# Graph attention by row chains over 128 runs of consecutive edges instead of one-hot matmuls over items

## What is computed

```python
h = x @ W                                    # per node, 256 wide
e = leaky_relu(al_s[src] + al_d[dst], 0.2)   # a score per edge and head
m = segment_max(e, dst)
ex = exp(e - m[dst])
denom = segment_sum(ex, dst)
out = segment_sum(h[src] * ex / denom[dst], dst) + b
```

## Time and profile before

| | us |
|---|---|
| median of 3 runs | 7049.85 |
| lowest and highest run | 7016.26 and 7051.68 |
| span of the profiled execution | 7015.4 |
| attention, layer 1 (1659 to 4269) | 2610 |
| close_first | 148 |
| attention, layer 2 (4417 to 6911) | 2494 |
| close_last | 105 |

### The profile page before, as it was taken

One profiled execution on the slowest core, in us unless ns is written; L12 is line 12 of the kernel. 1 busy time (PEld: TensorE's weight loads), 2 busy tenths in 40 slices (PEclk: granted clock), 3 DMA queues, 4 the chain that ended last, 5 costly groups with the idle time before them and its releaser, 6 DMA issues. The chain is left out here.

```text
span 7015.4 us, 84308 instructions
## 1 busy us (share of the span) xinstructions
PE 4539.2 (65%) x21954; PEld 3343.3 (48%) x21954; DVE 4230.7 (60%) x11585; ACT 2593.8 (37%) x7475; POOL 3741.4 (53%) x3828
## 2 busy tenths in 40 slices
PE   6776999995555555555555558466666666666662
PEld 4554777774444444444444445344444444444441
DVE  8997876665555555555555558555555555555557
ACT  7983222221444444444444446222222222222221
POOL 1334432233666666666666660566666666666661
PEclk9998999997777777777777779677777777777776
DMA  9997343333434434444444444444434344333446
GB/s 338 373 376 286 115 155 114 110 113 95 115 113 120 116 114 117 117 118 116 113 119 116 114 118 131 120 116 115 118 112 117 113 118 118 113 115 112 118 116 237
DMA packets 391446, 997.85 MB, mean 142 GB/s; under 512 B 106626, under 2 KB 199094, under 8 KB 378502
## 3 DMA queue, kind: packets, MB, share of 16 engines
q0 software_dynamic: 175200, 469.15, 24.7%
q1 hardware_dynamic: 205798, 471.33, 19.5%
q10 hardware_dynamic: 10048, 52.70, 1.9%
HBM read 804.88 MB, written 187.99 MB: 142 GB/s over the span
## 5 line engine op out<-in xcount | busy, mean ns | idle before, releaser
L247 POOL DMA_INDIRECT rows<-table_d,idx x3328 | 3217.8, 967 | 2077.7 <-issue 884.9
L489 DVE TENSOR_TENSOR acc<-acc,pG 128x264 f32 (+1 forms) x3328 | 1414.1, 425 | 1928.5 <-DMA rows_d<-begin_e 890.8
L290 PE MATMUL pG<-rows,onehot 128*128 128x264 f32 (+1 forms) x6656 | 2357.3, 502 | 308.7 <-issue 226.6
L290 PEld LDWEIGHTS pG<-rows,onehot 128*128 128x128 f32 x6656 | 1543.7, 248 | 922.4 <-issue 568.4
L350 ACT ACTIVATE onehot<-pQ 128x1024 f32<-128x1024 f32 (+1 forms) x512 | 442.4, 864 | 2223.5 <-DMA g2b<-in_g_b 1562.6
L357 ACT ACTIVATE rows<-rows 128x64 f32<-128x64 f32 (+1 forms) x4480 | 1251.4, 367 | 4.2
L264 PE MATMUL pQ<-k_nrow,drow 128*128 128x128 bf16 x3328 | 326.5, 248 | 638.9 <-ACT onehot L350 636.9
L271 PE MATMUL pS<-adt,onehotT 128*128 x3328 | 294.7, 171 | 544.7 <-issue 533.7
L264 PEld LDWEIGHTS pQ<-k_nrow,drow 128*128 128x128 bf16 x3328 | 250.0, 111 | 658.4 <-ACT onehot L350 647.5
L945 PE MATMUL pH<-hT_pre,w1h 128*128 128x256 f32 x1568 | 412.5, 419 | 137.9 <-ACT hT_pre L805 111.9
L271 PEld LDWEIGHTS pS<-adt,onehotT 128*128 128x128 bf16 x3328 | 219.1, 97 | 573.7 <-issue 535.0
(11 more groups left out here) (323 smaller groups left out, 5131.2 us busy)
## 6 DMA issues: line engine op xcount, KB each, us to landing
onehotT<-drow_d SPq DMA_DIRECT2D x128, 832.0 KB
ea<-in_ea SPq DMA_DIRECT2D x98, 768.0 KB
rows_d<-run SPq DMA_DIRECT2D x97, 768.0 KB
rows<-table_d,idx POOLq DMA_INDIRECT x3328
pre_d<-pre ACTq DMA_DIRECT2D x49, 1024.0 KB
pre_in<-pre_d SPq DMA_DIRECT2D x49, 1024.0 KB
hrow_c<-table_d SPq DMA_DIRECT2D x98, 256.0 KB
tab<-tab_d SPq DMA_DIRECT2D x64, 260.0 KB
```

Of the source, the lines that this page charges most:

```text
L247: g.indirect_dma_start(out=rows[:, at.par, k, 0:XF + H], out_offset=None, in_=table, in_offset=bass.IndirectOffsetOnAxis(ap=idx[:, at.par, ...
L290: mm = pe.matmul(pG[(k + 2 * at.par) % 4][:, 0:W], onehot[:, k, :], rows[:, at.par, k, :], start=True, stop=True)
L489: v.tensor_tensor(to, to, pG[(k + 2 * at.par) % 4][:, 0:W], ALU.add).then_inc(added, 1)
```

## The change

Both attention layers are computed in another way, and what only the old way needed goes.

**The layout.** Partition p gets the edges p*1563 to p*1563 + 1562, so step k of a "row chain" handles one edge in each of the 128 runs. The 1563 steps are cut into 58 groups: 23, then 54 of 28, then 14, 7 and 7. `rows` is a ring of four slots of one group each.

**The steps of a group.** POOL gathers one column of 128 rows per step (1563 gathers per layer, the index column in SBUF for good) and waits once per group, for the slot. DVE `maxima` computes the scores, a forward and a backward scan per head for the maximum, and the exponent. ACT takes the exponential. The rows are weighed: in layer 1, 20 of 28 by DVE in fours, both inputs in SBUF, and 8 by ACT; in layer 2 all by ACT. Then DVE `chain_rows`: one scalar_tensor_tensor per step, running row = running row before * same + row, read from one PSUM bank and written to the next, in a ring of six banks, each behind the one before. ACT copies two banks at a time back over the rows in SBUF, and SP stores the group to HBM (`sums1`, `sums2`). The last edge of a node then holds its sum.

**Ends of runs.** A node that spans a border of two runs is fixed at the end of the layer: the last rows of all runs go through small matmuls, and one indirect gather and one scatter mend the first node of each run.

**Around it.** `acc` in SBUF is gone: `close_first` and `close_last` fetch the sums from HBM with 98 gathers each (`Shares`), in chunks of 14 tiles with two buffers, and the softmax division moves into the chunks. The destination scores are scattered to the first edge of each node (98 small scatters in `node_mlp` for layer 1, 98 in `close_first` for layer 2, after the arrays are zeroed) and spread along the run by a scan. Item lists, tables and their stores are gone from `edge_chains` and `node_mlp`; PE has nearly no work in `attention`. The table rows carry 2H scores.

The core of the diff:

```diff
+GROUP = 28
+TAPER = (14, 7, 7)
+SLOTS = 4
...
+        body = self.EA - sum(TAPER)
+        sizes = [body % GROUP] * (body % GROUP > 0) + [GROUP] * (body // GROUP) + list(TAPER)
+        self.groups = []
+        for n, size in enumerate(sizes):
+            self.groups.append(Group(n, sum(sizes[:n]), size, sizes))
...
+    by_vector = [0 if H == 1 else min(g.size // 4 * 4, 4 * max(1, round(0.72 * g.size / 4))) for g in groups]
+    duos = [-(-g.size // 2) for g in groups]
+    first_duo = [sum(duos[:g.n]) for g in groups]
+    by_scalar = [g.size - n for g, n in zip(groups, by_vector)]
...
+            for g in groups:
+                sp.wait_ge(copied, first_duo[g.n] + duos[g.n])
+                sp.dma_start(outv[:, g.first * W:g.end * W],
+                             rows[:, g.slot, 0:g.size, :].rearrange("p k w -> p (k w)")).then_inc(stored[g.slot], 16)
...
+                if g.use:
+                    p.wait_ge(stored[g.slot], 16 * g.use)
+                    p.wait_ge(zm_ready, g.n - SLOTS + 2)
+                    p.wait_ge(fa_ready, g.n - SLOTS + 1)
+                for k in range(g.size):
+                    e = g.first + k
+                    p.indirect_dma_start(
+                        out=rows[:, g.slot, k, :], out_offset=None, in_=table,
+                        in_offset=bass.IndirectOffsetOnAxis(ap=keep["src"][:, e:e + 1], axis=0),
...
+                left = list(range(by_vector[g.n], g.size))
+                ahead = 4 if H == 1 else 0
+                for k in left[:ahead]:
+                    weigh(k)
+                left = left[ahead:]
+                for d in range(duos[g.n]):
+                    n = min(2, g.size - 2 * d)
+                    a.wait_ge(chained, min(g.first + 2 * d + 3, g.end))
+                    bank = (first_duo[g.n] + d) % 3 * 2
+                    a.activation(here[:, 2 * d:2 * d + n, 0:V], pC[:, bank:bank + n, 0:V], ACT.Copy).then_inc(copied, 1)
+                    for k in left[:2]:
+                        weigh(k)
+                    left = left[2:]
+            a.wait_ge(exponents, 2)
+            a.activation(flows[:, :, :], flows[:, :, :], ACT.Exp).then_inc(flows_ready, 1)
+            a.activation(old[:, :], old[:, :], ACT.Exp).then_inc(flows_ready, 1)
...
+            def destination_scores():
+                v.wait_ge(first_in, 16)
+                v.wait_ge(own_in, 16)
+                link(v.tensor_copy(ad[:, 0, :], own[:, V:W]))
+                for h in range(H):
+                    link(v.tensor_tensor_scan(ad[:, :, h], keep["same"][:, :], ad[:, :, h], 0.0, ALU.mult, ALU.add))
...
+            def maxima(g):
+                here, n = rows[:, g.slot, 0:g.size, :], g.size
+                prev = rows[:, groups[g.n - 1].slot, groups[g.n - 1].size - 1, :]
+                v.wait_ge(gath_in[g.slot], g.landed)
+                link(v.tensor_tensor(z[:, 0:n, :], here[:, :, XF:V], ad[:, g.first:g.end, :], ALU.add))
+                link(v.scalar_tensor_tensor(out=z[:, 0:n, :], in0=z[:, 0:n, :], scalar=0.2, in1=z[:, 0:n, :],
+                                            op0=ALU.mult, op1=ALU.max))
+                for h in range(H):
+                    start = prev[:, V + h:V + h + 1] if g.n else -BIG
+                    link(v.tensor_tensor_scan(fw[:, h, 0:n], keep["off"][:, g.first:g.end], z[:, 0:n, h], start, ALU.add, ALU.max))
+                for h in range(H):
+                    link(v.tensor_tensor_scan(here[:, ::-1, V + h], keep["off"][:, g.first + 1:g.end + 1][:, ::-1],
+                                              fw[:, h, 0:n][:, ::-1], -BIG, ALU.add, ALU.max))
+                v.tensor_tensor(zm[:, 0:n, :], z[:, 0:n, :], here[:, :, V:W], ALU.subtract).then_inc(zm_ready, 1)
+                if g.n:
+                    v.scalar_tensor_tensor(out=fa[:, :], in0=prev[:, V:W], scalar=keep["off"][:, g.first:g.first + 1],
+                                           in1=here[:, 0, V:W], op0=ALU.add, op1=ALU.subtract).then_inc(fa_ready, 1)
...
+            def weigh(g):
+                here = rows[:, g.slot, 0:g.size, :]
+                v.wait_ge(w_ready, g.n + 1)
+                for k in range(0, by_vector[g.n], 4):
+                    part = here[:, k:k + 4, 0:XF].rearrange("p k (h d) -> p k h d", h=H)
+                    by = here[:, k:k + 4, XF:V].unsqueeze(3).to_broadcast([P, 4, H, D])
+                    v.tensor_tensor(part, part, by, ALU.mult).then_inc(weighed_dve, 1)
...
+            def carry(g, prev, row, to):
+                v.wait_ge(fade_ready, g.n)
+                if H == 1:
+                    v.scalar_tensor_tensor(out=to, in0=prev, scalar=fade[:, 0:1], in1=row, op0=ALU.mult,
+                                           op1=ALU.add).then_inc(chained, 1)
                     return
+                v.tensor_tensor(before[:, 0:XF].rearrange("p (h d) -> p h d", h=H), prev[:, 0:XF].rearrange("p (h d) -> p h d", h=H),
+                                fade[:, :].unsqueeze(2).to_broadcast([P, H, D]), ALU.mult).then_inc(vec, 1)
+                link.n += 1
+                link(v.tensor_tensor(before[:, XF:V], prev[:, XF:V], fade[:, :], ALU.mult))
+                v.tensor_tensor(to, row, before[:, :], ALU.add).then_inc(chained, 1)
...
+                    if k < n:
+                        v.wait_ge(weighed_dve, sum(by_vector[:g.n]) // 4 + (k // 4 + 1))
+                    else:
+                        v.wait_ge(weighed_act, sum(by_scalar[:g.n]) + (k - n + 1))
+                    if e:
+                        v.wait_ge(chained, e)
+                    duo = first_duo[g.n] + k // 2
+                    if k == 0 and g.n:
+                        v.wait_ge(copied, duo)
+                    elif k % 2 == 0 and duo >= 3:
+                        v.wait_ge(copied, duo - 2)
+                    row, to = here[:, k, 0:V], running(g, k)
+                    if e == 0:
+                        v.tensor_copy(to, row).then_inc(chained, 1)
+                    elif k == 0:
+                        before_it = groups[g.n - 1]
+                        carry(g, running(before_it, before_it.size - 1), row, to)
+                    else:
+                        v.scalar_tensor_tensor(out=to, in0=running(g, k - 1), scalar=keep["same"][:, e:e + 1], in1=row,
+                                               op0=ALU.mult, op1=ALU.add).then_inc(chained, 1)
...
+    def gather(self, g, n):
+
+        for u in range(2):
+            j = 2 * n + u
+            g.indirect_dma_start(
+                out=self.acc[:, n // PER % 2, j % self.CH, :], out_offset=None, in_=self.rows,
+                in_offset=bass.IndirectOffsetOnAxis(ap=self.keep["gather"][:, 2, j:j + 1], axis=0),
+            ).then_inc(self.acc_in[n // PER % 2], 16)
...
+            g.wait_ge(keep["sums_out"], 16)
+            for n in range(2 * PER):
+                sh.gather(g, n)
+            for n in range(NS):
+                if n + 2 * PER < NS:
+                    g.wait_ge(summed, n + 1)
+                    sh.gather(g, n + 2 * PER)
+                g.wait_ge(ald_ready, n + 1)
+                for j in (2 * n, 2 * n + 1):
+                    g.indirect_dma_start(
+                        out=dr["first2"], out_offset=bass.IndirectOffsetOnAxis(ap=keep["first"][:, j:j + 1], axis=0),
+                        in_=keep["ald"][:, j, 0:1], in_offset=None).then_inc(keep["first_out"], 16)
...
+            g.wait_ge(keep["sums_out"], 32)
+            for n in range(NS):
+                if n >= 2 * PER:
+                    g.wait_ge(summed, 2 * (n - 2 * PER) + 2)
+                sh.gather(g, n)
```

More of the change, by code:

```diff
@@ L1977, in step @@
[L1977 to L1991 removed]
+            sh.own_scores(v, chain)
```

1254 lines of the change are left out of this document (411 added, 843 removed).

## The result

The changed kernel takes 7168.7 us (median of four runs, 7152.4 to 7191.2) where the kernel before takes 7035.3 us in the same comparison: a ratio of 1.019, with a 95% interval of 1.016 to 1.022. It is slower by 1.9%; the forecast was 6440 us. Two different things went wrong with the forecast, and the experiments separate them. (The text says TensorE for PE, VectorE for DVE, ScalarE for ACT, SyncE for SP, and POOL as the profile does.)

A forecast was written before the change was run, and what follows sets the result against it. The prediction took a PE, DVE, PE, ACT loop, slower than the gathers alone, to bound attention. From 7015.4 us, -330 - 483 + 135 + 68 - 5 + 5 gave 6410, or 6440 as the runs' median; range 6110 to 6780.

The forecast's parts named there:

- The step that failed is the first: Old attention stages: a PE, DVE, PE, ACT loop over two buffers runs 20 to 25% slower than the gathers alone.
- The second step: New attention stages: PE's, DVE's and ACT's work per group, 30.7 and at most 24 us, hides under 35.1 us of gathers.
- Attention 1: Attention stage of layer 1: 2280 us in place of 2610, so -330 us.
- Attention 2: Attention stage of layer 2: 2011 us in place of 2494, so -483 us.
- Contention with the weighing: Attention: DVE instructions with two SBUF inputs and small ones delay gathers, 268 us in layer 1, 22 in layer 2.
- `close_first`: Stage after attention 1: 98 gathers and 98 scatters on POOL, 246 us, make it 283 us, +135.
- `close_last`: Last stage: 98 gathers beside DVE's two-input work and more DMA bytes, +68 us.
- `node_mlp`: Second stage: PE stays the bound and covers POOL's added scatters; a longer start by the zeros costs +5 us.
- `edge_chains`: First stage: loses 39 gathers and some 15 small DVE instructions, -5 us.
- The slots come back late, and POOL waits for `stored`: Rival, attention: long stores return slots late, so POOL waits per group; about 6900 us, chance 0.03.
- The crowded DMA: Rival, attention: stores of running rows crowd DMA and slow every gather; 7800 us, chance 0.07.
- the first rival: Rival, attention and closing stages: gathers lose nothing to the weighing; 6080 us, chance 0.14.

The follow-up runs named there:

- before_again: The kernel before, nothing edited, on a further chip without late semaphore updates: 6222.0 us.
- after_again: The changed kernel, nothing edited, on a further chip without late semaphore updates: 6260.7 us, 1.010 of the kernel before.
- no_scatters: The changed kernel without the 98 scatters of close_first: 6236.6 us in all, close_first 281 us.
- weigh_8_deep: The changed kernel with 8 rows per layer 1 group weighed by VectorE, and close_first loads eight pairs ahead, before stores: 6128.6 us, 0.992 of the kernel before.

## Why the prediction was wrong

**The step that failed is the first.** It read the distance between 40.8 and 39.0 us per batch and 32.6 us of gathers as "a loop PE, DVE, PE, ACT over two buffers that runs 20 to 25% slower than the gathers alone", a property of the old algorithm that the change takes away. It came with the chip, in the shape of late updates: with updates in time the same loop takes 33.2 and 33.0 us. The change could win only its 100 gathers fewer per layer, 125 us in each, less what contention takes. The rows to see it in were there. The earlier trace rows puts 415.6 us of POOL's idle time, and the earlier trace rows 890.8 us of VectorE's, down to `rows_d<-begin_e`, a transfer of the first stage that had landed long before. I used the 416 us as a wait for PE. A releaser that can't be one means that the real one's update was recorded much later than its end, or not at all, and it should have been followed with single waits.

**The second step is "covered by the gathers in both layers".** The cycle was sized well: 30.7 us forecast for layer 1 and 30.6 measured, "at most 24" and 23.7 in layer 2, a chain step 0.63 us and 0.60. Where updates are late it is 45 or 62 us in two of three groups of layer 2, and 31 and 24 us are no measure of what covers what. The prediction took durations from the trace of before, but no latency from an instruction's end to its update. That trace had it in both attention stages, where 1067 of TensorE's 2540 recorded changes are late, and to a lesser degree in `node_mlp` (42 of 483, beside 7 of 506 in `before_again`). With it at nothing, the forecast priced the new stages for a chip without late updates and compared them with old ones measured with them.

Term by term, first on the result's execution, then with updates in time (`after_again` less `before_again`):
- Attention 1: -330 forecast; -166; -13. The new stage was forecast at 2280 us and takes 2159 where updates are in time, mainly because contention takes half of what was priced; the old one was 438 us longer in my profile than it is there.
- Attention 2: -483; -71; -154. Forecast 2011, taken 2004: right to 0.4%.
- Contention with the weighing: 4.8 us per group of layer 1 forecast, 2.3 measured (37.37 less 35.04), of which the five weighings bring 2.1 and the small instructions the rest; 22 us in layer 2 forecast, nothing measured.
- `close_first` +135; +176; +155. Right by its number and wrong by its reason: not POOL's 246 us but the order and depth of SyncE's loads, as `no_scatters` and `weigh_8_deep` show.
- `close_last` +68; +74; +74. Right: its gathers last 1.27 us in the mean beside VectorE's additions, 98 x (1.27 + 0.30) = 154 us of the 178.
- `node_mlp` +5; +116; +7. Right where updates are in time. Where they are late, TensorE's first product of a step ends at 1213.9 and VectorE gets its update at 1217.3, and in the changed kernel this delay is 3.4 us in most steps where it was 1.5 before, with POOL's two scatters now issued in that stretch. That they cause it was not tried on such a chip.
- `edge_chains` -5; +34; -36. Chance, in both kernels: it takes 637 to 639 us in five of the profiled executions after the result and 670 to 678 in the others, with a granted clock of 0.92 or 0.81 over its first 640 us. The 36 us flatter the changed kernel in the pair above; without them it is 69 us behind, not 33. The timed executions fall in the same two groups: in the slower one the changed kernel takes 6296 us in the mean beside 6223, in the faster one 6258 beside 6186, 1.012 both times. `weigh_8_deep` is at 0.991 in either group, on both chips.

**The rivals.** "The slots come back late, and POOL waits for `stored`" had 3% and 6900 us: it is the form that the stage took, with 733 us of such waits. Its mechanism, long stores, was not the cause. The crowded DMA did not come: at 207 GB/s the gathers of layer 2 kept their pitch of 1.25 us. (By its own terms, with the 290 us counted already taken off, that rival is slower than before from a pitch of 1.54 us on, not 1.45.) The gathers did lose time to the weighing, so the first rival fell, and the chain step took 0.60 us, so the second did. No rival had the baseline itself as something that might not be the kernel's own, so 0.91 for faster was far too much.

## What to carry to other kernels

Before a wait in a profile is called a property of the code, look at whether its releaser could have been one, and whether the instruction that must have released it had ended long before; if so, latency is being measured, and a change that keeps as many handshakes can keep it too. Before recorded semaphore changes are used for this, compare their number with that of the instructions that make them: a change without a record looks like a late one. Compare the sum of the one thing that both versions must do (here 26 gathers at 1.25 us) with a second execution, on another chip, before the gap is promised as a gain. Where an engine's queue carries loads and stores in one order, a load behind a store that waits for the end of the work is the first thing to move: with more loads in flight it gave 40 us of 297 here.

## What was not expected of the hardware

- Semaphore updates can come late (8.5 us after ScalarE's copy ended) in executions on some chips, and come within 0.02 us of the instruction's end, but for a few, on four others, for the same program: 7016 to 7052 us and 6182 to 6226 us for the kernel before. In such stretches ScalarE starts independent instructions of 0.35 us at 0.70 or 1.40 us. The same traces lack more than half of the semaphore changes, and both go with stages in which POOL issues indirect DMAs. What causes it stays open.
- An indirect DMA of POOL beside a series of VectorE instructions with two SBUF inputs waits for one of them at most (1.05 us of 1.22), not for the series.
- 128-row gathers keep 1.25 us beside stores of the same size, with DMA at 0.62 in the mean (layer 2 of `after_again`).
